# A two-stage graph layer: SyncE runs ahead, ScalarE stores, and the attention values are made in the gather stage

## The reference, cut to what matters

```
h      = relu(layernorm(x))
k, q   = h @ tokeys.T, h @ toqueries.T
dots   = sum(k[src] * relations[rel] * q[src], axis=1) / 128
values = exp(dots)
values = values / rowsum[(src, rel)]         # rowsum: sum of values over edges of one (src, rel)
output[(src, rel)] += values * h[dst]        # over all edges
out    = x + relu(sum over rel of output[(:, rel)] @ (comps @ bases)[rel])
```

## Time and profile before

| | |
|---|---|
| median of 3 runs | 3081.46 us (3079.8 to 3084.72) |
| profiled execution, its own time | 3066.26 us |
| profiled execution, span | 3064.5 us |
| PE / DVE / ACT / POOL busy | 51% / 44% / 15% / 54% |
| mean granted TensorE clock | 0.673 |

### The profile page before, as it was taken

The page is one execution under the profiler, slowest core; times in us unless marked ns, Lnnn a source line. Parts: engine busy times, 40 slices in busy tenths (PEclk is TensorE's granted clock), DMA queues, the critical chain, the costliest instruction groups (busy, mean ns, idle before and its releaser), DMA issues.

```text
span 3064.5 us, 32426 instructions
## 1 busy us (share of the span) xinstructions
PE 1549.4 (51%) x9121; PEld 1129.2 (37%) x9122; DVE 1354.7 (44%) x2385; ACT 462.7 (15%) x918; POOL 1651.2 (54%) x1804
## 2 busy tenths in 40 slices
PE   4999932444344454534454443544444444544435
PEld 3666621233233333323333332333333333333324
DVE  7999934334243433424343342434334243433423
ACT  4666611000010100001010000101000010101000
POOL 3444444655646465555646565564655556464653
PEclk8999965656666665666666566666656566666667
DMA  5444411111111111111111111111111111111111
GB/s 154 156 155 155 155 55 32 46 41 42 45 36 45 36 46 39 43 42 41 45 36 45 38 44 43 40 45 37 45 38 43 44 39 45 36 46 36 45 42 29
DMA packets 99825, 170.47 MB, mean 56 GB/s; under 512 B 32491, under 2 KB 48612, under 8 KB 99575
## 3 DMA queue, kind: packets, MB, share of 16 engines
q0 software_dynamic: 51776, 104.48, 13.1%
q1 hardware_dynamic: 47672, 65.57, 6.3%
q10 hardware_dynamic: 352, 0.14, 0.0%
HBM read 112.24 MB, written 59.59 MB: 56 GB/s over the span
## 4 chain that ended last, share of the span: by engine, by line
another core or an unknown queue 40%; issue 21%; DVE 20%; PE 14%; SPq 2%; DMA 2%; DVEq 1%; ACT 0%; POOLq 0%; ACTq 0%
PE bank L1199 6%; DVE arena L825 4%; DVE CX L790 3%; PE bank L1184 2%; DVE stage L768 2%; DVE WC L801 2%; DVE pay_all L784 1%; PE bank L1152 1%; PE bank L1276 1%; DVE OHR L766 1%; PE bank L1319 1%; DMA RL<-bucket_streams 1%; DVE pay_all L815 1%; PE bank L1307 1%
## 5 line engine op out<-in xcount | busy, mean ns | idle before, releaser
L492 POOL DMA_INDIRECT arena<-Z_messages,IDX x1568 | 1483.0, 946 | 1137.4 <-issue 955.1
L1319 PE MATMUL bank<-arena 128*128 128x128 f32 x3528 | 695.2, 353 | 733.1 <-issue 724.9
L1319 PEld LDWEIGHTS bank<-arena 128*128 128x128 f32 x3528 | 632.5, 264 | 797.3 <-issue 795.3
L799 DVE TENSOR_SCALAR WC<-bank 128x128 f32<-128x128 f32 x49 | 14.3, 292 | 1150.5 <-remote 1149.2
L1101 ACT COPY pay_all<-bank 128x1024 bf16<-128x1024 bf16 x147 | 108.0, 807 | 2136.6 <-remote 2059.9
L1307 PE MATMUL bank<-pay_all 128*128 128x256 bf16 x882 | 179.8, 347 | 310.9 <-DVE arena L825 249.1
L825 DVE TENSOR_TENSOR arena<-stage,bank 128x512 f32<-128x512 bf16 x441 | 268.9, 681 | 12.1 <-remote 7.8
L768 DVE TENSOR_TENSOR stage<-bank,NLF 128x4608 bf16<-128x4608 f32 x49 | 242.4, 4948 | 0.0
L1307 PEld LDWEIGHTS bank<-pay_all 128*128 128x128 bf16 x882 | 86.6, 113 | 386.2 <-DVE arena L825 297.4
L1276 PE MATMUL bank<-stage,OHR 128*128 128x512 bf16 (+1 forms) x441 | 198.5, 618 | 3.2 <-DVE arena L825 3.1
L1199 PE MATMUL bank<-WT,HT 128*128 128x512 f32 x392 | 186.3, 615 | 0.0
(11 more groups left out here) (211 smaller groups left out, 1715.5 us busy)
## 6 DMA issues: line engine op xcount, KB each, us to landing
Z_messages<-stage SPq DMA_DIRECT2D x192, 256.0 KB
arena<-Z_messages,IDX POOLq DMA_INDIRECT x1568
X<-in_x SPq DMA_DIRECT2D x4, 768.0 KB, 12.8
out<-O SPq DMA_DIRECT2D x48, 64.0 KB
bucket_streams<-bucket_streams SPq DMA_DIRECT2D x97, 18.0 KB
arena<-in_L_gnn_bases_w SPq DMA_DIRECT2D x1, 1024.0 KB, 15.0
bucket_streams<-arena SPq DMA_DIRECT2D x1, 882.0 KB
RL<-bucket_streams SPq DMA_DIRECT2D x49, 18.0 KB
```

Of the source, the lines that this page charges most:

```text
L492: g.indirect_dma_start(Gbuf[par][:, k, :], None, Z, bass.IndirectOffsetOnAxis(IDX[turn][:, k:k + 1], 0))\
L1319: return t_.matmul(bank[2][:, 0:EMB], OW[:, k, :], Gbuf[par][:, k, :], start=start, stop=stop)
```

## The change

- The keys, queries, their product and V of bucket b+1 leave the routing stage. They are made in `stepb(b)` of the gather stage, from the node features that are normalised again there. The new functions are `value_normalise`, `value_relu`, `value_product` (DVE), `value_turn`, `value_keys`, `value_dots` (PE) and `value_exp` (ACT). They use parts of PSUM bank 2, columns 128 on, while `aggregate` writes columns 0 to 127, and `aggregate` waits for the values of the bucket after the current one.
- SP no longer waits for a record load to land or for an output to be finished. It joins both halves ahead, and stops only for joins and for a free record buffer.
- ACT stores the outputs, at the end of `bucket(b)`, and copies the shared tile of bucket b-1 there instead of bucket b.

```diff
@@ SyncE
-                def bucket(b, par, rl_total):
-                    if dyn(b) or b < NB:
+                def bucket(b, par):
+                    sp.wait_ge(s["join"], b * 32 + 16)
+                    sp.sem_inc(s["sp_go"], 1)
+                    if dyn(b) or 1 <= b < NB - 1:
+                        join(b + 1, 0)
+                        sp.wait_ge(s["join"], b * 32 + 32)
                         sp.sem_inc(s["sp_go"], 1)
-                        load_records(b, par)
-                    if dyn(b) or b + 1 < NB:
-                        sp.wait_ge(rl[par], rl_total)
-                        sp.sem_inc(s["sp_go"], 1)
                         join(b + 1, 1)
                     if dyn(b) or b >= 2:
-                        store_out(b - 2, par)
+                        sp.wait_ge(s["rl_t"], b - 1)
+                        sp.sem_inc(s["sp_go"], 1)
+                    load_records(b, par)
...
@@ GpSimd
-                g.tensor_tensor(PR[par][:], SO[:, 0:P], SO[:, P:2 * P], ALU.mult).then_inc(s["prod"], 1)
...
@@ VectorE
+            def value_normalise(b):
+                if dyn(b) or b >= 1:
+                    dve.wait_ge(s["nth"], b)
+                v.tensor_scalar(H[:], X[:, bass.ds(b, 1), :]..., rstd[:, bass.ds(b, 1)],
+                                shift[:, bass.ds(b, 1)], ALU.mult, ALU.add).then_inc(s["nh"], 1)
+            def value_relu(b):
+                dve.wait_ge(s["nth"], b + 1)
+                v.tensor_scalar(HT[0][:], NHT, 0.0, None, ALU.max).then_inc(s["nht"], 1)
+            def value_product(b):
+                dve.wait_ge(s["nkq"], b + 1)
+                v.tensor_copy(SO[:, 0:P], NKQ[:, P:2 * P]).then_inc(s["nq"], 1)
+                dve.wait_ge(s["nq"], b + 1)
+                v.tensor_tensor(PR[0][:], NKQ[:, 0:P], SO[:, 0:P], ALU.mult).then_inc(s["npr"], 1)
...
                 def stepb(b, par, o_total, turn):
+                        value_normalise(b + 1)
                         records(b + 1)
                         gather_index(b + 1, turn)
+                        value_relu(b + 1)
                         own_counts(b)
+                        value_product(b + 1)
                         weights(b, par)
...
@@ ScalarE
-                a.copy(SO[:], bank[6][:, 0:2 * P]).then_inc(s["so_sb"], 1)
...
+            def value_exp(b):
+                act.wait_ge(s["nv"], b + 1)
+                a.activation(V[:, bass.ds(b, 1), :]..., bank[2][:, P:P + R], ACT.Exp,
+                             scale=1.0 / EMB).then_inc(s["v"], 1)
+                def store_out(b, par, n=P):
+                    act.wait_ge(s["o"], b + 1)
+                    act.sem_inc(s["act_go"], 1)
+                    a.dma_start(out[bass.ds(b * P, n), :], O[par][0:n, :]).then_inc(ost[par], 16)
...
+                        value_exp(b + 1)
                         spread_relations(b + 1, 1 - par)
-                        shared_tile(b, par)
+                    if dyn(b) or b >= 1:
+                        shared_tile(b - 1, 1 - par)
+                    if dyn(b) or b >= 2:
+                        store_out(b - 2, par)
...
@@ TensorE
-            def keys_queries(i, par):
+            def messages(i, par):
                 pe.wait_ge(s["ht"], i + 1)
-                t_.matmul(bank[6][:, 0:P], KQT[:, 0, :], HT[par][:], start=True, stop=True)
-                t_.matmul(bank[6][:, P:2 * P], KQT[:, 1, :], HT[par][:], start=True, stop=True)
...
+            def value_turn(b, free):
+                pe.wait_ge(s["nh"], b + 1)
+                t_.transpose(NHT, H[:], identf[:]).then_inc(s["nth"], 1)
+            def value_keys(b):
+                pe.wait_ge(s["nht"], b + 1)
+                t_.matmul(NKQ[:, 0:P], KQT[:, 0, :], HT[0][:], start=True, stop=True)
+                t_.matmul(NKQ[:, P:2 * P], KQT[:, 1, :], HT[0][:], start=True, stop=True).then_inc(s["nkq"], 1)
+            def value_dots(b):
+                pe.wait_ge(s["npr"], b + 1)
+                t_.matmul(NV, PR[0][:], relT[:], start=True, stop=True).then_inc(s["nv"], 1)
...
                 def aggregate(b, par):
+                    if dyn(b) or b + 2 < NB:
+                        pe.wait_ge(s["v"], b + 3)
...
                 def stepb(b, par, rl_total):
                         turn_records(b + 1, 1 - par, rl_total)
+                        value_turn(b + 1, b - 1 if dyn(b) or b >= 2 else None)
                         tables(b, par)
+                        value_keys(b + 1)
                         sum_counts(b)
+                        value_dots(b + 1)
                         aggregate(b - 1, 1 - par)
                         lookups(b)
```

More of the change, by code:

```diff
@@ L214, in program @@
             dup dense loc stat varr stdd ln ohb s8 s8_sb bt bt_sb ncount own fold half m_sum rk ohs idxw mx pos pay d_mm d_sb rec_mm rec_sb scat
-            h th ht so_mm so_sb prod z_mm z_sb zst0 zst1 zrow v ends ends_mm nt nt_total nt_mm nt_row shared act_go join sp_go marks_sb marks_st
+            h th ht nh nth nht nkq nq npr nv z_mm z_sb zst0 zst1 zrow v ends ends_mm nt nt_total nt_mm nt_row shared act_go join sp_go marks_sb marks_st
             rl0 rl1 rl_t ri dec nlf idx inv rrf ohn ohr ord vr cnt cm cx cs masks x3 w w3 bd tp oht lk ow gat0 gat1 land0 land1 land2 land3 acc o ost0 ost1
@@ L350, in bucket @@
                         join(b + 1, 1)
                     if dyn(b) or b >= 2:
-                        store_out(b - 2, par)
-                def store_out(b, par, n=P):
-                    sp.wait_ge(s["o"], b + 1)
-                    sp.dma_start(out[bass.ds(b * P, n), :], O[par][0:n, :]).then_inc(ost[par], 16)
+                        sp.wait_ge(s["rl_t"], b - 1)
+                        sp.sem_inc(s["sp_go"], 1)
+                    load_records(b, par)
+                    if not dyn(b) and b == 0:
+                        sp.wait_ge(rl[0], 16)
+                        join(1, 0)
+                        sp.wait_ge(s["join"], 32)
+                        join(1, 1)
@@ L359, in _ @@
                 join(0, 1)
-                bucket(0, 0, 16)
-                bucket(1, 1, 16)
+                bucket(0, 0)
+                bucket(1, 1)
                 with sp.Fori(0, (NB - 1) // 2 - 1) as j:
-                    bucket(j * 2 + 2, 0, j * 16 + 32)
-                    bucket(j * 2 + 3, 1, j * 16 + 32)
-                bucket(NB - 1, 0, None)
-                store_out(NB - 2, 1)
-                store_out(NB - 1, 0, LASTN)
+                    bucket(j * 2 + 2, 0)
+                    bucket(j * 2 + 3, 1)
@@ L368, in _ @@
+                bucket(NB - 1, 0)
                 sp.wait_ge(ost[0], 16 * ((NB + 1) // 2))
@@ L869, in _ @@
                 gather_index(0, 0)
+                value_normalise(0)
+                value_relu(0)
+                value_product(0)
                 tables(0, 0)
@@ L879, in _ @@
             with dve.If(bad > 0):
+                value_normalise(0)
+                value_relu(0)
+                value_product(0)
+                with dve.Fori(1, NB) as b:
+                    value_normalise(b)
+                    value_relu(b)
+                    value_product(b)
+                dve.wait_ge(s["v"], NB)
                 dve.wait_ge(s["marks_st"], 48)
@@ L1022, in copy_rec @@
                 a.activation(REC[par][:], bank[3][0:NS, 0:WIN], ACT.Copy, bias=BIG * 4097).then_inc(s["rec_sb"], 1)
-                if dyn(i) or i < NB:
-                    a.activation(V[:, bass.ds(i, 1), :].rearrange("p a r -> p (a r)"), bank[3][:, 256:256 + R],
-                                 ACT.Exp, scale=1.0 / EMB).then_inc(s["v"], 1)
-                else:
-                    a.copy(stats[0:1, 0, 0:1], stats[0:1, 0, 1:2]).then_inc(s["v"], 1)
             def copy_z(i, par, lo, hi):
@@ L1103, in bucket @@
                     if dyn(b) or b + 1 < NB:
+                        value_exp(b + 1)
                         spread_relations(b + 1, 1 - par)
-                        shared_tile(b, par)
+                    if dyn(b) or b >= 1:
+                        shared_tile(b - 1, 1 - par)
+                    if dyn(b) or b >= 2:
+                        store_out(b - 2, par)
+                value_exp(0)
                 spread_relations(0, 0)
@@ L1113, in _ @@
                 bucket(NB - 1, 0)
+                store_out(NB - 2, 1)
+                store_out(NB - 1, 0, LASTN)
             with act.If(bad > 0):
+                value_exp(0)
+                with act.Fori(1, NB) as b:
+                    value_exp(b)
                 with act.Fori(0, NCOL) as t:
@@ L1349, in _ @@
                 turn_records(0, 0, 16)
+                value_turn(0, None)
+                value_keys(0)
+                value_dots(0)
                 stepb(0, 0, 16)
@@ L1358, in _ @@
             with pe.If(bad > 0):
+                value_turn(0, None)
+                value_keys(0)
+                value_dots(0)
+                with pe.Fori(1, NB) as b:
+                    value_turn(b, None)
+                    value_keys(b)
```

(1 more changed line is left out.)

59 lines of the change are left out of this document (24 added, 35 removed).

## The result

The changed kernel takes 3289.94 us (median of 4 runs, 3288.13 to 3292.26), the kernel before 3080.63 us beside it. The ratio is 1.0678, with a 95% interval of 1.066 to 1.0697. The profiled execution took 3292.26 us, with a span of 3290.5.

The account below looks back on a forecast made before the run. PE was taken to bound the routing stage, and additions released at S the gather stage. 3066 - 17 + 45 x 5.2 (234) + 7 = 3290, plus 15 for the median: 3305 us; range 2895 to 3350, likeliest case 3224 to 3350.

Parts of the forecast that it names:

- routing stage: PE loses 0.64 us a step, DVE becomes the bound after 0.36: 48 steps gain 17 us, from nothing to 31.
- first buckets: Buckets 0 and 1: tables(0) waits for the values of bucket 0; adds 7 us, 0 to 20.
- SyncE's part, stores: Gather stage: earlier joins and loads on SP, output stores on ACT; taken as 0, stores at most 0.7 us a bucket.
- later tile: Gather stage: shared tile of b-1 done at S + 10.0, covered by additions that end at S + 13.5.
- S: Moment in a gather burst when PE's completions all become visible, some 6.2 us after its last gather starts; claimed fixed.
- 72 rows of additions: PE's additions in aggregate(b-1), now all behind S: 10.92 us after a pause, 9.08 us in a warm PE.
- Rivals 3 and 4: Rival 3, gather stage: earlier records bring acc forward, 3.2 us a period less, 2917 us, chance 0.16. Rival 4 has its own line.
- rival 4: Gather stage: acc always done in time, POOL never pauses, 13.5 us a period less: 2443 us, chance 0.09.
- The chain behind S: Gather stage: product, dots and exponential take 2.6 us, then all additions: 13.5 us instead of 8.26, +5.2 us a period.
- Rival 2: Gather stage: values and shared tile hidden, leaving the routing gain, 3064 us, or no change, 3075 to 3087; chances 0.09, 0.05.
- the 15 us between the profiled execution and the median: Whole kernel: runs' median 3081 against the profiled 3066, added to the sum of 3290 to give 3305.
- Rival 1: Gather stage: values hidden, only the later shared tile costs, 1.2 us a period: 3125 us, chance 0.08.

Follow-up runs that it names:

- e2: Changed kernel with the SyncE and ScalarE part undone (loads, output stores and shared tile as before), values still in the gather stage: 3305.64 us, ratio 1.073.
- e6: Kernel before with SyncE's joins and loads ahead and ScalarE storing outputs, shared tile of bucket b as before: 3080.71 us, ratio 1.0044.
- e1: Kernel before with the SyncE and ScalarE part alone: joins and loads ahead, ScalarE's stores, shared tile of bucket b-1: 3143.43 us, ratio 1.0201.
- e4: Changed kernel with 17 of the 18 transposes of tables(b) left out from the third bucket on: 2983.21 us in one run.
- e7: Changed kernel with value_dots(b+1) behind aggregate(b-1), which waits for value_product alone, and value_exp at the end of ScalarE's bucket: 3222.55 us, ratio 1.0503.
- e5: Changed kernel with values of bucket b+1 behind lookups(b), aggregate not waiting for them, and shared tile of bucket b as before: 3081.71 us, ratio 1.0037.
- e8: Changed kernel with 16 small extra multiplications ahead of the nine of tables(b): 3324.83 us in one run.
- e9: Kernel before with only the values moved, to the gather stage behind lookups(b): 2366.19 us, ratio 0.9889, beside 2392.98.
- e12: Kernel before with the orders of e9 and e11 together: 2365.45 us, ratio 0.9883, beside 2393.41.
- e11: Kernel before with the 18 transposes of bucket b put behind aggregate(b-1) in PE's order: 2392.70 us, ratio 1.0001.
- e10: Kernel before with only the values moved, to the gather stage in one piece ahead of tables(b): 2367.40 us, ratio 0.9892.

## Why the prediction was right

The forecast was 3305 us, from a sum of 3290 for the profiled execution. Step by step, measured as in the two tables:

| step | forecast | measured |
|---|---|---|
| routing stage | -17 | -26.8 |
| first buckets | +7 | +9.0 |
| SyncE's part, stores | 0 | -0.5% in the change (e2), +0.4% alone (e6) |
| later tile | covered | covered; 1.3 to 1.75 us a period where it is not (e1) |
| additions start behind S | 2.6 us | 2.66 us |
| 72 rows of additions | 10.92 us | 10.49 us |
| S to the end of the additions, before | 8.26 us | 7.72 us |
| a period | +5.2 us | +5.27 us by the two profiles, +4.9 by the medians |
| number of periods | 45 | 46 |
| last burst to the end | 0 | +1.4 |
| sum | 3290 | 3292.26 |

The +4.9 comes from the 209 us between the medians: (209.3 + 26.8 - 9.0 - 1.4) / 46.

**The fixed S** carried the argument, and for the bursts of 31 to 33 gathers it held: in every kernel with the slow phase and all its transposes, DVE's sums start, in the mean, 6.2 to 8.2 us behind the last gather, with records turned 4 us or 13 us into the burst. Rivals 3 and 4 fell on this. The earlier transposes (10.4 us into the burst and not 17.7) brought nothing forward. The last bursts differ. After SyncE's last join at 2960.65 ACT sees the transposes sooner from burst to burst, 3.7 us behind the last gather in that of 2988.7 and 14.5 us ahead of it in that of 3161.9. The sums still come 5.1 us behind it there, and the additions end at 17.5. In e1, whose last join is at 2835.15, the sums come sooner too, from the burst of 2914.4 on between 2.3 us behind the last gather and 1.7 ahead. SyncE's joins may have a share in the slow phase, but no run tests it, and in the kernel before the first burst behind the last join (2941.1) shows nothing of it.

**What was wrong about S.** Against rival 4 the prediction says that in the double burst of buckets 0 and 1 the slow phase lasted as long as the gathers. The completions there do not wait for the end of the gathers. First the kernel before, whose last gather of the double burst starts at 501.75, then the changed kernel, with its last at 474.93:

```profile
434.89 1.18 PE L1286 MATMUL bank<-identb,ORD 128*128 128x128 bf16 x18
476.62 2.20 ACT L1101 COPY pay_all<-bank 128x1024 bf16<-128x1024 bf16 x3 [51.87 <-issue]
487.12 0.29 DVE L799 TENSOR_SCALAR WC<-bank 128x128 f32<-128x128 f32 x1 [48.79 <-remote]
```

```profile
409.92 1.80 PE L1327 MATMUL bank<-identb,ORD 128*128 128x128 bf16 x18
...
470.55 0.29 DVE L730 COPY SO<-bank 128x128 f32<-128x128 f32 x1 [57.17 <-remote]
481.16 0.29 DVE L805 TENSOR_SCALAR WC<-bank 128x128 f32<-128x128 f32 x1 [9.99 <-remote]
```

Before, the 18 transposes are seen 40.5 us behind the end of their rows, 2.25 us a row, and the four rows of sums 10.5 us later, 2.6 a row, all of it ahead of the last gather. In the changed kernel it is 46.8 us for the transposes (ACT starts at 458.48, still ahead of the last gather), 12.1 for four rows of keys and queries and 10.6 for four of sums. So completions come one row each 2 to 3 us, as in e4, and the end of a burst releases what is left. My estimate from these rows: in a burst of 32 of the changed kernel, transposes that end 11.5 us into it would be seen at 52 to 58 us, behind S at 45. That is why S looked fixed. It held because 18 rows at this pace do not fit into 32 gathers, which the prediction did not work out, and in this it was lucky.

**The chain behind S** was right in both parts, and e7 and e5 part them: without dots and exponential the period is 1.5 us shorter, and with all of it elsewhere and the tile as before (e5) it is within 0.6 us of e6. Rival 2, values hidden, is what e5 shows for another order of the same work.

**Mis-sized terms.** The routing stage gave 26.8 us and not 17. The wait was right (0.35 of 0.36 us), but DVE's L542 also got 0.12 us shorter, so DVE did not stop PE after 0.36 us of the 0.64: a step is 0.56 us shorter (6.41 us, where the prediction had 6.6). That was inside my upper end of 31. Which of the removed instructions had slowed L542 was not tried. I took one bucket's 8.26 us for the additions before, where the mean is 7.7, and 10.92 for 10.49; the first made the forecast period 0.54 us too short and the second 0.43 us too long, so they cancel almost wholly, which was luck. The additions' time goes with the granted clock of PE in it: 0.79 and then 1.00 in the 9.08 us of bucket 1, 0.50 (1.2 GHz) and then 0.94 in the 10.92 us of the last aggregation, 0.62 and then 1.00 in the 9.90 us shown above. And I took the 15 us between the profiled execution and the median for a property of the kernel. They were not: beside e5 to e8 the kernel before had a median of 3067.44, and the changed kernel's median lies 2 us below its profiled execution. Without that term the forecast would have been 3290. The sum also has 45 periods where there are 46, 5 us too few.

**Rival 1's price**, 1.2 us, was a little low (e1: 1.3 to 1.75). I had S + 10.3 for the next burst, and e1 has 16.55 - 6.38 = S + 10.2; but the mean of before is S + 8.5 and not the 9.06 of the bucket that I read.

**The page of the Trainium skill** that the prediction named (the Trainium skill, Perfetto Trace Analysis, Tensor Engine Instruction: the end of a PE row is computed) fits the changed kernel as well: its transposes end by their row at 1583.50, and ACT starts at 1617.08. The other one (the Trainium skill, Perfetto Trace Analysis, DMA Optimizations: inputs and outputs on different engines may help in a loop) is not borne out here: e6, which does this together with the earlier joins and loads, has a ratio of 1.0044.

## What to carry to other kernels

When work moves from a stage with a full engine to one with idle engines, ask at which moment its results can be seen, and what will wait for them. Here a chain of 2.7 us cost 5.3 us a bucket, because all 72 rows of additions, a third of which had been issued ahead of S, were put behind it; the same work behind `lookups` cost 0.6. Where two releases of a waiting engine lie close together (additions at 13.9, tile at 15.7), moving the one without the other only changes the name of the wait.

## What the runs showed of the hardware

- In the runs of 3067 us and more, completions of PE come late while gathers are issued, and later the more rows stand ahead of them: with 16 small rows more, a completion that had been seen at once was seen 31 us later (e8); with 17 fewer, one that had come 6 us behind the last gather came 28 us ahead of it (e4). In the double burst 18 transposes were seen 40.5 and 46.8 us late and the next four rows 10.5 to 12.1 us behind, 2.3 to 3.0 us a row. The single additions that PE starts in this time stand mostly 2.1 to 2.8 us apart. The mechanism stays unknown.
- Whether this happens at all changed from one set of runs to another. The same kernel before took 3067 to 3082 us on two chips and 2393 us on two others, and there POOL issued its gathers every 1.25 us without a pause in e9 to e12 (the kernel before has no profile there; e11 has one, and the same time). Chip and time of the run changed together, so which of them decides stays open. Both the 6.8% loss here and the wait that I analysed were seen on chips of the first kind alone. On the others the value move, at the place of e9, e10 or e12, gains 1.1 to 1.2%.
- On the first kind no order that was run beats the kernel before; the best with the values moved is e5 at 1.0037.
